# Layer 0's row-max products over 64 rows, with ones brought by transfer and stacks built in halves

## The reference

```python
def _L0_attn_ref(x, w_project, w_out):
    b, s, d = x.shape
    qkv = jnp.einsum('bsd,od->bso', x, w_project)
    qkv = qkv.reshape(b, s, 3, NUM_HEAD, HEAD_DIM)
    qkv = jnp.transpose(qkv, (2, 0, 3, 1, 4))
    q, k, v = (qkv[0], qkv[1], qkv[2])
    att = jnp.einsum('bhqd,bhkd->bhqk', q, k) / math.sqrt(HEAD_DIM)
    causal = jnp.triu(jnp.ones((s, s), dtype=bool), k=1)
    att = jnp.where(causal[None, None, :, :], jnp.float32(-1000000000.0), att)
    att = jax.nn.softmax(att, axis=-1)
    out = jnp.einsum('bhqk,bhkd->bhqd', att, v)
    out = jnp.transpose(out, (0, 2, 1, 3)).reshape(b, s, d)
    return jnp.einsum('bsd,od->bso', out, w_out)

x = L0_attn_x
x = x + _L0_attn_ref(_layernorm(x, axis=-1), L0_attn_w_project, L0_attn_w_out)
```

## Time and profile before

| | |
|---|---|
| median of three runs | 1406.98 us (1406.31 to 1411.0) |
| the profiled execution | 1404.72 us |
| its span | 1403.0 us, 19467 instructions |
| PE busy | 1098.4 us, 78% |
| DVE busy | 1117.2 us, 80% |
| ACT busy | 453.4 us, 32% |
| POOL busy | 271.3 us, 19% |
| L537 (row-max products) | 256 products, 71.1 us |
| L744 (reductions of them) | 160, 104.6 us |

### The profile page before, as it was taken

One profiled execution on the slowest core, in us unless ns is written; L12 is line 12 of the kernel. 1 busy time (PEld: TensorE's weight loads), 2 busy tenths in 40 slices (PEclk: granted clock), 3 DMA queues, 4 the chain that ended last, 5 costly groups with the idle time before them and its releaser, 6 DMA issues. The chain is left out here.

```text
span 1403.0 us, 19467 instructions
## 1 busy us (share of the span) xinstructions
PE 1098.4 (78%) x6516; PEld 580.4 (41%) x6576; DVE 1117.2 (80%) x2046; ACT 453.4 (32%) x708; POOL 271.3 (19%) x257
## 2 busy tenths in 40 slices
PE   0687878885587978878758888787877677999996
PEld 0243434443333434334323354363455344556564
DVE  7479696874389998999866888897899899677775
ACT  1044343432243242342314423404212133444443
POOL 7024241434224433234330000000000000000000
PEclk9699999998788989899869999998989899999999
DMA  3512121110000100101000000010010100000001
GB/s 90 120 51 67 54 57 63 46 32 24 14 0 0 39 0 0 37 0 38 0 15 1 1 18 15 1 31 0 7 23 14 26 27 12 1 1 0 0 1 60
DMA packets 36263, 34.66 MB, mean 25 GB/s; under 512 B 8024, under 2 KB 32856, under 8 KB 36192
## 3 DMA queue, kind: packets, MB, share of 16 engines
q1 hardware_dynamic: 36192, 33.75, 8.6%
HBM read 27.28 MB, written 6.29 MB: 24 GB/s over the span
## 5 line engine op out<-in xcount | busy, mean ns | idle before, releaser
L744 DVE TENSOR_REDUCE bm<-ps 128x4 f32<-128x512 f32 x160 | 104.6, 672 | 16.8 <-PE ps L541 15.5
L666 ACT ACTIVATE pt<-ps 128x1024 f32<-128x1024 f32 (+1 forms) x96 | 83.0, 881 | 98.7 <-PE ps L587 97.3
L920 POOL TENSOR_TENSOR wt<-lg,mid 128x2048 f32<-128x2048 f32 x16 | 75.3, 4709 | 185.4 <-DVE mid L1112 185.4
L537 PE MATMUL ps<-ks,qs 96*128 96x512 bf16 (+3 forms) x256 | 71.1, 324 | 44.6 <-DVE bm L744 28.0
L1034 ACT ACTIVATE wt<-wt 128x2048 f32<-128x2048 f32 x16 | 30.6, 1915 | 193.9 <-POOL wt L920 193.9
L1487 DVE TENSOR_TENSOR qk_lo<-ps,qk_hi 128x512 bf16<-128x512 f32 x80 | 54.9, 687 | 42.6 <-ACT qk_hi L1389 42.0
L815 POOL TENSOR_SCALAR rstd<-mv 128x4 f32<-128x4 f32 x12 | 2.7, 229 | 437.2 <-DVE mv L1496 217.1
L1656 PE MATMUL ps<-ew_hi,it_hi 128*128 128x256 bf16 x256 | 70.4, 275 | 17.1 <-DVE it_lo L1760 17.1
L1744 DVE SCALAR_TENSOR_TENSOR g<-g,ps 128x512 f32<-128x512 f32 x64 | 43.8, 685 | 46.0 <-ACT g L1694 45.7
L481 POOL TENSOR_SCALAR_AFFINE_SELECT pt<-pt 128x256 f32<-128x256 f32 (+1 forms) x96 | 46.8, 490 | 154.2 <-ACT pt L666 154.2
L1389 ACT ACTIVATE qk_hi<-ps 128x512 bf16<-128x512 f32 x80 | 47.7, 596 | 88.5 <-PE ps L1280 88.5
(11 more groups left out here) (228 smaller groups left out, 3003.9 us busy)
## 6 DMA issues: line engine op xcount, KB each, us to landing
qs<-scratch_q SPq DMA_DIRECT2D x64, 64.0 KB, 2.6
ks<-scratch_k SPq DMA_DIRECT2D x64, 64.0 KB, 2.6
q_next<-in_w_qkv SPq DMA_DIRECT2D x4, 768.0 KB, 4.6
X<-in_x SPq DMA_DIRECT2D x4, 512.0 KB, 7.0
w_next<-in_router_w SPq DMA_DIRECT2D x4, 512.0 KB, 4.1
w_next<-in_expert_w SPq DMA_DIRECT2D x4, 512.0 KB, 5.1
p_next<-in_w_proj SPq DMA_DIRECT2D x4, 512.0 KB, 5.9
out<-X SPq DMA_DIRECT2D x4, 512.0 KB, 4.6
```

The costliest lines, as they stand in the source:

```text
L537: pe.matmul(ps[:, o + P * i:o + P * (i + w)], qs[0:SHIFT, h, P * j:P * (j + 1)], ks[0:SHIFT, h, P * k0:P * (k0 + w)], start=(i == 0), stop ...
L666: act.activation(pt[kt][:, heads[0]:heads[-1] + 1, :], src, ACT.Exp).then_inc(s_exp, 1)
L744: ins = dve.tensor_reduce(bm[:, 2 * g + i // 5, 4 * (i % 5):4 * (i % 5) + 4], src.rearrange("p (k q) -> p k q", k=4), AX_X, ALU.max)
L920: pool.tensor_tensor(wt[:, :, :], lg[t % 2][:, :, :], over_experts(mid), ALU.subtract).then_inc(s_mid, 1)
```

## The change

`SHIFT` becomes `STK` = 64: the stacks have 66 rows, no zero rows, and the row-max product goes over 64 rows. The ones are made once by GpSimd as a small tile and brought to rows 64 and 65 of `ks` by two transfers of SP. GpSimd no longer writes the three long memsets; its memsets of `stage` come behind `rstd`. DVE makes `w_lo` behind `xn`. TensorE, ScalarE and DVE wait for less at their beginning: TensorE waits for `wsplit_hi` and `wsplit_lo` only ahead of the first projection, and for the ones, `const_v` and `load_wo` after `START`. The projections come in the order 0, 2, 1, 3. The copies to scratch are made by halves of the heads, two halves of four transfers of 128 KB with a semaphore for each half; a group's stacks wait for its half alone. In the start, SP issues the stacks of queries and ScalarE those of keys.

```diff
-SHIFT = 96
+SHIFT = STK
...
-PREPARE = [("xT", 0), ("xT", 1), ("qk", 0), ("qk", 1), ("qk", 2), ("qk", 3)]
+QK_ORDER = (0, 2, 1, 3)
+PREPARE = [("xT", 0), ("xT", 1)] + [("qk", m) for m in QK_ORDER]
...
+        ones_row = st.sb("ones_row", [H0 * G, P], BF16)
...
+        def stack_rows(eng, g, which):
+
+            heads = slice(HG * g, HG * (g + 1))
+            for n in which:
+                scr, dst, hi_lo_rows = ((scratch_q, qs, ((0, 2), (1, 3))), (scratch_k, ks, ((0, 1), (2, 3))))[n]
+                for part, rows in enumerate(hi_lo_rows):
+                    for r in rows:
+                        eng.dma_start(dst[HD0 * r:HD0 * (r + 1), heads, :],
+                                      scr[part].rearrange("(h d) t -> d h t", d=HD0)[:, heads, :]).then_inc(s_stk[g], 16)
...
-                def copy_parts(b, qk_work):
-
-                    for g in range(NG):
+                def copy_parts(b, qk_work, half_):
+
+                    for g in (2 * half_, 2 * half_ + 1):
...
+                        m = 2 * n + half_
+                        sp.wait_ge(s_taken, qk_work[m] + 1)
                         for part, buf in enumerate((qk_hi, qk_lo)):
-
-                            sp.wait_ge(s_taken, qk_work[2 * n + 1] + 1)
-                            sp.dma_start(scr[part].rearrange("(m p) t -> p m t", p=P),
-                                         buf[:, 2 * n:2 * n + 2, :]).then_inc(s_scr, 16)
-
-                    wait_alone(sp, s_scr, 64 * b + 64, passed_sp)
+                            sp.dma_start(scr[part, P * half_:P * (half_ + 1), :], buf[:, m, :]).then_inc(s_scr[half_], 16)
 
                 def stack_group(b, g):
 
+                    wait_alone(sp, s_scr[g // 2], 64 * b + 64, passed_sp)
...
-                copy_parts(0, [START.index(("qk", m)) for m in range(4)])
-                for g in range(NG):
-                    stack_group(0, g)
+                sp.wait_ge(const, 1)
+                for r in (SHIFT, SHIFT + 1):
+                    sp.dma_start(ks[r:r + 1, :, :].rearrange("o h (j q) -> o (h j) q", q=P), ones_row[:, :]
+                                 ).then_inc(s_ones, 16)
+                for half_ in range(2):
+                    copy_parts(0, [START.index(("qk", m)) for m in range(4)], half_)
+                    wait_alone(sp, s_scr[half_], 64, passed_sp)
+                    for g in (2 * half_, 2 * half_ + 1):
+                        stack_rows(sp, g, (0,))
                 shift_group(0, 0, START.index(("turn", 0)))
...
             def _(pool):
-                for e in range(E):
-                    pool.memset(glob["stage"][0:4, 0, D * e:D * (e + 1)], -e * ZERO_STEP).then_inc(rows_set, 1)
-                pool.memset(glob["stage"][0:4, 1, :], 0.0).then_inc(rows_set, 1)
+                pool.memset(ones_row[:, :], 1.0).then_inc(const, 1)
...
                 root(0)
                 pool.wait_ge(s_rstd, 2)
-                pool.memset(ks[SHIFT:SHIFT + 2, :, :], 1.0).then_inc(const, 1)
-                pool.wait_ge(const, 6)
-                pool.memset(ks[STK:SHIFT, :, :], 0.0).then_inc(const, 1)
-                pool.wait_ge(const, 7)
-                pool.memset(qs[STK:SHIFT, :, :], 0.0).then_inc(const, 1)
+                for e in range(E):
+                    pool.memset(glob["stage"][0:4, 0, D * e:D * (e + 1)], -e * ZERO_STEP).then_inc(rows_set, 1)
+                pool.memset(glob["stage"][0:4, 1, :], 0.0).then_inc(rows_set, 1)
...
             def _(pe):
-                pe.wait_ge(wsplit_hi, 1)
-                pe.wait_ge(wsplit_lo, 1)
-                pe.wait_ge(const, 5)
-                pe.wait_ge(const_v, 3)
-                pe.wait_ge(load_wo, 16 * HG)
+                pe.wait_ge(const, 6)
...
                 for n, (kind, arg) in enumerate(START):
-                    if n == len(PREPARE):
-
-                        pe.wait_ge(const, 8)
+                    if n == KC:
+                        pe.wait_ge(wsplit_hi, 1)
+                        pe.wait_ge(wsplit_lo, 1)
                     work(0, n, n % 2, kind, arg, 0)
+
+                pe.wait_ge(s_ones, 32)
+                pe.wait_ge(const_v, 3)
+                pe.wait_ge(load_wo, 16 * HG)
...
                 for n, (kind, arg) in enumerate(START):
                     take(0, n, n % 2, kind, arg)
+                for half_ in range(2):
+                    act.wait_ge(s_scr[half_], 64)
+                    for g in (2 * half_, 2 * half_ + 1):
+                        stack_rows(act, g, (1,))
...
                 statistics(0)
-                dve.wait_ge(load, 16)
-                dve.wait_ge(wsplit_hi, 1)
-                dve.tensor_tensor(w_lo[:, :, :], w_f[:, :, :], w_hi[:, :, :], ALU.subtract).then_inc(wsplit_lo, 1)
...
                 normalised(0)
+                dve.wait_ge(load, 16)
+                dve.wait_ge(wsplit_hi, 1)
+                dve.tensor_tensor(w_lo[:, :, :], w_f[:, :, :], w_hi[:, :, :], ALU.subtract).then_inc(wsplit_lo, 1)
```

More of the change, by code:

```diff
@@ L279, in layer0_attention @@
         s_xn, s_xhi, s_xlo, s_qkhi = st.sem("xn0s"), st.sem("xhi0"), st.sem("xlo0"), st.sem("qkhi")
-        s_scr, s_stk = st.sem("scr"), [st.sem(f"stack{g}") for g in range(NG)]
+        s_scr, s_stk = [st.sem(f"scr{n}") for n in (0, 1)], [st.sem(f"stack{g}") for g in range(NG)]
+        s_ones = st.sem("ones_rows")
         s_work, s_taken, s_mx = st.sem("bank_work"), st.sem("bank_taken"), st.sem("row_max")
@@ L342, in copy_parts @@
                     for n, scr in enumerate((scratch_q, scratch_k)):
+                        m = 2 * n + half_
+                        sp.wait_ge(s_taken, qk_work[m] + 1)
                         for part, buf in enumerate((qk_hi, qk_lo)):
-                            sp.wait_ge(s_taken, qk_work[2 * n + 1] + 1)
-                            sp.dma_start(scr[part].rearrange("(m p) t -> p m t", p=P),
-                                         buf[:, 2 * n:2 * n + 2, :]).then_inc(s_scr, 16)
-                    wait_alone(sp, s_scr, 64 * b + 64, passed_sp)
+                            sp.dma_start(scr[part, P * half_:P * (half_ + 1), :], buf[:, m, :]).then_inc(s_scr[half_], 16)
                 def stack_group(b, g):
+                    wait_alone(sp, s_scr[g // 2], 64 * b + 64, passed_sp)
                     reach(sp, s_st, 6 * (NG * (b - 1) + g + 1))
[L355 to L361, removed]
+                    stack_rows(sp, g, (0, 1))
                 def shift_group(t, g, turned):
@@ L392, in batch @@
                             if g == 0:
-                                copy_parts(b + 1, [n + work.index(("qk", m)) for m in range(4)])
+                                for half_ in range(2):
+                                    copy_parts(b + 1, [n + work.index(("qk", m)) for m in range(4)], half_)
                             stack_group(b + 1, g)
@@ L413, in _ @@
                 pool.memset(sel[:, :], 0.0).then_inc(const, 1)
-                pool.wait_ge(const, 3)
+                pool.wait_ge(const, 4)
                 pool.affine_select(out=maskneg[:, :], in_=maskneg[:, :], compare_op=ALU.is_ge, fill=NEG, base=0,
@@ L639, in _ @@
                 act.activation(w_hi[:, :, :], w_f[:, :, :], ACT.Copy).then_inc(wsplit_hi, 1)
-                act.wait_ge(const_v, 3)
                 def take(b, n, parity, kind, arg):
@@ L647, in take @@
                         act.wait_ge(s_work, n + 1)
-                        reach(act, s_scr, 64 * b)
+                        reach(act, s_scr[arg % 2], 64 * b)
                         act.activation(qk_hi[:, arg, :], bank(MAXB[parity]), ACT.Copy,
@@ L717, in take @@
                     elif kind == "qk":
-                        dve.wait_ge(s_qkhi, 4 * ahead + arg + 1)
-                        reach(dve, s_scr, 64 * ahead)
+                        dve.wait_ge(s_qkhi, 4 * ahead + QK_ORDER.index(arg) + 1)
+                        reach(dve, s_scr[arg % 2], 64 * ahead)
                         ins = dve.scalar_tensor_tensor(qk_lo[:, arg, :], src, (HD0 ** -0.5 if arg < 2 else 1.0),
```

## The result

The changed kernel takes 1459.39 us, the median of four runs (1449.27 to 1469.65), against 1407.37 for the kernel before in the same comparison (1406.31 to 1411.0): a ratio of 1.0365, interval 1.029 to 1.044. The forecast was 1402. The profiled execution of after is its longest run, 1469.65 us with a span of 1467.6, 64.6 us above the span of before, so the losses read from it are some 10 us larger than the medians'.

What follows compares the result with a forecast made beforehand. Bounds taken: at the start, xn held by GpSimd memsets, then the chain through memory; TensorE in first groups, DVE in later ones. 19.2 + 4.6 - 3.7 - 7.7 - 7.5 = 4.9 us faster: 1402 us, range 1390 to 1412.

Steps and rivals of the forecast that it cites:

- (a): Start: without the three long memsets xn ends at 12.0 us instead of 31.22; 19.2 us gained (17.2 to 20.0).
- (b): Start: copies to scratch by halves (3.0 us earlier) and stacks on two queues (1.6); 4.6 us gained (3.5 to 5.0).
- The 1.6 us for the second queue: Start: four of group 0's eight stack issues on another queue shorten its issue; 1.6 us gained.
- The DMA engines were 41% busy in that stretch: Start, stack transfers: doubling the rate was said to nearly fill the DMA engines; the ground for taking 1.6 us.
- the rival in which it stays up: TensorE's gap before the first row-max: clock does not fall, first stage gains 1.6 us; about 1397 us, chance 0.14.
- (c): Row-max product over 64 rows: tile changes cost 0.19 us a pair at 2.4 GHz; losses of 3.7, 7.7 and 7.5 us.
- The rival in which 64 rows cost nothing: Row-max products: 64-row products bring no price, so the change has only its start; 1383 us, chance 0.08.
- The first stage: First row-max stage, 20 units at 1.2 GHz: 19.8 us against 16.1, TensorE its bound, 3.7 us lost.
- 8 x 0.096 = 0.77 us per group: Ten later groups with row-max work: eight tile changes each not covered by idle TensorE; 7.7 us lost (5 to 15).
- 1.9 us for each first group: Four first groups, bound by TensorE: part of 16 pairs' 3.1 us is covered by waits; 7.5 us lost (4 to 12).
- The slower rival: Groups: TensorE becomes the bound, 16 pairs bring 3.1 us against 2.6 idle; 23 us slower, 1430 us, chance 0.12.
- 43 + 3.7: Loss if all 14 groups pay 3.1 us in full (43 us), plus the first row-max stage's 3.7 us.

Runs made afterwards that it cites:

- experiment 6: The change with 96 and 98 rows kept, GpSimd writing the zero rows behind xn: 1385.61 us, ratio 0.9831 to the kernel before.
- experiment 12: Experiment 7 with all first stacks issued on SP's queue, none by ScalarE: 1383.21 us, ratio 0.982.
- experiment 2: The kernel before with its row-max products over 64 rows, zero rows and 98-row scores kept: 1443.73 us, ratio 1.0283.
- experiment 9: Experiment 6 plus a 4-row, 16-column product adding zeros in each pair of row-max and mask products (512 changes of tile): 1412.51 us, ratio 1.0026.
- experiment 5: The kernel before with its row-max product over 65 rows instead of 96, nothing else changed: 1419.14 us against 1409.08, ratio 1.0078.
- experiment 10: The change with 65-row row-max products and 67-row scores, plus a 4-row product adding zeros in each row-max and mask pair: 1473.88 us, ratio 1.0471.
- experiment 11: Experiment 6 with row-max products over 64 rows, and stacks and scores padded with zero rows to 128: 1406.32 us, ratio 0.9982.
- experiment 7: Experiment 6 with stacks padded with zero rows to 128, so scores go over 128 rows: 1382.72 us, ratio 0.9823.

## Why the prediction was wrong, point by point

**(a), the zero rows: right.** The first transpose came at 11.68 us, 19.7 earlier than before, where 19.2 was taken and 12 to 12.5 expected. The doubt was whether xn is held once per memset. With short memsets beside it xn was only slowed, to 1.66 us, and GpSimd's eight memsets to 2.64 from 2.07. With none beside it (experiment 6) xn took 1.38. w_lo cost nothing.

**(b), halves and queues: 3.7 us where 4.6 stood, and one of its two terms was nothing.** From the first transpose to the first row-max it took 18.41 us instead of 22.08. The 1.6 us for the second queue were not there; that the total came near was in part luck, as the halves gave some 3.7 us where 3.0 stood. The DMA rows of after, from 20 to 31 us (KB each, median us from issue to landing):

```profile
ks<-scratch_k ACTq DMA_DIRECT2D x8, 64.0 KB, 5.3
qs<-scratch_q SPq DMA_DIRECT2D x8, 64.0 KB, 4.7
```

On one queue in before they took 2.8 and 2.9. Two queues issue the stacks of groups 0 and 1 side by side, and each transfer takes nearly twice as long. Windows of after:

```profile
25.00:26.00 1.00, 0.00 (x0) 0.00 (x0) 0.00 (x0) 0.00 (x0) 0.00 (x0) 1.00 1.10 166
26.00:27.00 1.00, 0.00 (x0) 0.00 (x0) 0.00 (x0) 0.00 (x0) 0.00 (x0) 0.50 1.16 132
...
29.00:30.00 1.00, 0.00 (x0) 0.00 (x0) 0.00 (x0) 0.00 (x0) 0.00 (x0) 0.50 1.21 113
```

And of before, copies to scratch (43 to 44 us) and stacks, all on one queue:

```profile
43.00:44.00 1.00, 0.00 (x0) 0.00 (x0) 0.43 (x1) 0.53 (x1) 0.00 (x0) 1.00 0.86 296
...
50.00:51.00 1.00, 0.00 (x0) 0.00 (x0) 0.00 (x0) 0.00 (x0) 0.00 (x0) 0.50 0.46 138
...
58.00:60.00 2.00, 1.79 (x8) 0.73 (x9) 1.78 (x4) 0.00 (x0) 0.00 (x0) 0.50 1.16 131
```

The stacks moved 113 to 166 GB/s at shares over 1 in after and 120 to 138 at 0.41 to 0.48 in before. The step that failed is "The DMA engines were 41% busy in that stretch, so doubling the rate nearly fills them". The share is not a measure of room: with one queue, the same transfers moved 138 GB/s at 0.46 and 131 at 1.16. They ran at the stacks' own pace, while the copies to scratch reached 296 GB/s; what sets that pace the runs do not show. The Trainium skill, "DMA: Bandwidth & Descriptors", "Issuing engines are not separate DMA queues", says that starting transfers on several engines saves only the time of the issue; the trace and experiment 12, with one queue and the first row-max product at 29.89 us, agree.

**The clock in the start: right.** It fell to 0.50 at 26 us, within TensorE's gap before the first row-max, and the rival in which it stays up did not come.

**(c), the price of a change: right in kind and size.** The timeline of after at 1.2 GHz and at 2.4 GHz:

```profile
95.10 0.50 PE L541 MATMUL ps<-ks,qs 64*128 64x384 bf16 x1
95.53 0.29 PE L545 MATMUL ps<-maskneg,identb 128*128 128x128 bf16 x1
95.75 0.29 PE L541 MATMUL ps<-ks,qs 64*128 64x128 bf16 x1
```

```profile
168.62 0.39 PE L541 MATMUL ps<-ks,qs 64*128 64x512 bf16 x1
168.94 0.23 PE L545 MATMUL ps<-maskneg,identb 128*128 128x128 bf16 x1
169.10 0.39 PE L541 MATMUL ps<-ks,qs 64*128 64x512 bf16 x1
```

At 2.4 GHz 512 columns take 0.22 and 128 take 0.055; the steps are 0.32 and 0.16, so a change costs 0.10 each way. At 1.2 GHz the columns take 0.32 and 0.11, and the steps are 0.43 and 0.22: 0.11 each. That is 0.21 and 0.22 for a pair, where 0.19 and 0.23 stood, read from a 4-row product. The rival in which 64 rows cost nothing is out. The first stage took 20.25 us, forecast 19.8.

**(c), the groups: wrong, and here the prediction failed.** The terms that failed are "8 x 0.096 = 0.77 us per group" for the ten later groups and 1.9 us for each first group. Measured in the profiled run: 6.4 and 4.3. The working itself is not bad where its silent premise holds. In experiment 2 the clock stays up in six of the ten later groups, and they take 13.0 to 13.1 us, 0.5 more than before. The premise was that a granted clock of 1.00 in the groups belongs to the groups and stays whatever the products look like. It is an answer of the chip to those products. The prediction weighs the clock in one place only, the gap of the start, as if nothing but idle time of TensorE could lower it. The trace of before did not contradict that. Its one fall in the first group of batch 1, the 0.98 of the earlier trace rows and the 0.95 above, begins at 138.7 us, behind two waits of TensorE:

```profile
137.03 0.39 PE L537 MATMUL ps<-ks,qs 96*128 96x512 bf16 x1 [0.53 <-DVE mt_lo L734]
...
138.92 1.12 PE L509 MATMUL ps<-ident,xn 128*128 128x128 f32 x4 [1.44 <-DVE xn L708]
```

So the second way to lose the clock, by what the products are, could not be read from before; it took the changed kernel to show it. One reading of the rows was off beside this, without weight for the result: 141.0 to 166.2 us in the earlier trace rows is not one first group. That group lasts from 131.6 to 164.7 us, 33.1 us long, with TensorE busy 27.90 and DVE 21.04.

**The slower rival: right in its sign, too small by its mechanism.** It let TensorE become the bound at 2.4 GHz, with at most 3.1 us per group, 1430 at the end. TensorE did become the bound, but by the clock, which takes more than 3.1: the nine groups take 17.3 to 21.0 us. Where 32 changes per group meet TensorE mostly at full speed, nearly this rival's case, the loss is 26.9 us (experiment 9 against 6), not 43 + 3.7.

**What stays open.** The runs show that fewer rows, zero rows among them, and more changes of tile each lower the granted clock, and that together they do so far more. By what quantity the chip decides they do not show, and none is claimed. Nor do they show whether a change of tile counts by the time in which it leaves TensorE without columns or in another way.

## What to carry to other kernels

Zero rows in a contraction cost no time in the products and here kept the clock: in a stretch bound near TensorE, leave them, or pad to 128 rows, and try it, before trimming. Keep the memsets that write them off the opening chain. Read the granted clock group by group, before a change and after, and don't take a 1.00 for granted once the products change: most of the falls in experiments 2 and 5 lasted 3.4 us each, those of the change and of experiment 10 up to 37.5. The part worth keeping is the start: memsets of GpSimd that held DVE's opening instructions, moved behind them, and copies in halves together gave 23.5 us.

## What the hardware showed that was not expected

- The granted clock answered to the number of rows in products whose extra rows are zeros: 96 to 65 rows in one kind of product cost 10 us (experiment 5), 98 to 128 in another gave 19 us beside changes of tile (experiment 11) and nothing without them (experiment 7).
- A 1.2 GHz stretch lasted 37.6 us with TensorE busy in all of it, by the profile's modelled ends. That did not bring the clock back.
- Eight short memsets on GpSimd and four DVE instructions beside them slowed each other by 0.57 and 0.28 us. Before, four DVE instructions were held by three long memsets for 18 us.
- 64 KB stack transfers moved 113 to 146 GB/s from one queue and 113 to 166 from two, at DMA shares from 0.41 to over 1; copies of 256 KB reached 296 GB/s.
- A product of 65 rows follows and precedes 128-row products without a step; one of 64 rows costs 0.10 to 0.11 us on each side.
